# Four graph-attention layers on one core: an opening with gated loads, two reordered rounds, a smaller first piece in layer 3, and POOL converting one adjacency tile

## The reference

```python
x = _layernorm(x + _L0_gnn_ref(x, adj, W, a))          # 4 heads of 64, leaky slope 0.01, then elu
x = _layernorm(x + _L1_gnn_ref(x, adj, W, a1, a2))     # 4 heads of 64, leaky slope 0.2
x = _layernorm(x + _L2_gnn_ref(x, adj, W, ...))        # 1 head of 256, beside three dense branches and a gate
x = _layernorm(x + _L3_gnn_ref(x, adj, 4096, W, b, a)) # weights that depend on the source node alone
```

## Time and profile before

| what | value |
|---|---|
| median of 3 runs | 3027.12 us (3026.69 to 3028.43) |
| profiled execution, time | 3027.04 us |
| profiled execution, span | 3025.2 us |
| granted TensorE clock, mean | 0.992 |
| busy: PE, DVE, ACT, POOL | 2947.3, 2138.8, 1921.5, 1173.2 us |

### The profile page before, as it was taken

The page is one execution under the profiler, slowest core; times in us unless marked ns, Lnnn a source line. Parts: engine busy times, 40 slices in busy tenths (PEclk is TensorE's granted clock), DMA queues, the critical chain, the costliest instruction groups (busy, mean ns, idle before and its releaser), DMA issues.

```text
span 3025.2 us, 65221 instructions
## 1 busy us (share of the span) xinstructions
PE 2947.3 (97%) x24628; PEld 2580.8 (85%) x24628; DVE 2138.8 (71%) x3855; ACT 1921.5 (64%) x3414; POOL 1173.2 (39%) x1559
## 2 busy tenths in 40 slices
PE   7899999999989999999999999999999999989999
PEld 6899999999989999999998877888788878755555
DVE  5998888888988888888886556665666666562245
ACT  4777899999988999999995544454455444430000
POOL 0661385642226656564222023233333333444222
PEclk9999999999999999999999999999999999999999
DMA  8667100000100000000010000000000000000001
GB/s 289 203 206 246 60 15 11 14 11 15 61 12 15 11 11 14 11 14 11 15 34 12 4 1 4 4 1 4 1 4 4 1 1 1 2 1 1 0 14 42
DMA packets 41912, 104.55 MB, mean 35 GB/s; under 512 B 9856, under 2 KB 23424, under 8 KB 33536
## 3 DMA queue, kind: packets, MB, share of 16 engines
q1 hardware_dynamic: 39616, 101.61, 10.3%
q10 hardware_dynamic: 2112, 0.52, 0.1%
HBM read 97.73 MB, written 4.39 MB: 34 GB/s over the span
## 4 chain that ended last, share of the span: by engine, by line
PE 88%; DVE 5%; DMA 3%; ACT 2%; issue 2%; POOL 1%; SPq 0%; DVEq 0%; POOLq 0%; ACTq 0%
PE bank L1373 21%; PE bank L1370 21%; PE bank L1428 15%; PE bank L1466 13%; PE bank L1376 11%; DMA arena<-in_adj_dram 3%; PE bank L1301 2%; PE bank L1455 2%; PE bank L1442 1%; DVE rings L1797 1%; DVE arena L1717 1%; ACT above L967 1%; PE bank L1313 1%; PE bank L1351 1%; DVE rings L1792 1%
## 5 line engine op out<-in xcount | busy, mean ns | idle before, releaser
L1370 PE MATMUL bank<-values,rings 128*128 128x195 bf16 x8192 | 1413.3, 246 | 35.9 <-DVE rings L1800 24.0
L1373 PE MATMUL bank<-values,rings 128*128 128x195 bf16 x8192 | 1413.4, 249 | 0.0
L967 ACT ACTIVATE above<-srow,kpass 128x512 fp8e4<-128x512 f32 x2032 | 1280.1, 709 | 121.3 <-DVE rings L1800 114.6
L1370 PEld LDWEIGHTS bank<-values,rings 128*128 128x128 fp8e4 x8192 | 806.1, 98 | 45.1 <-issue 43.1
L1373 PEld LDWEIGHTS bank<-values,rings 128*128 128x128 fp8e4 x8192 | 788.7, 96 | 0.4
L1797 DVE TENSOR_TENSOR rings<-rings,above 128x512 uint32<-128x512 uint32 x512 | 399.6, 781 | 184.6 <-PE bank L1373 160.9
L1055 ACT ACTIVATE values<-srow,cmul 128x512 f32<-128x512 f32 x256 | 205.8, 814 | 411.2 <-PE bank L1466 410.3
L1800 DVE TENSOR_TENSOR rings<-rings 128x512 uint32<-128x512 uint32 x512 | 430.6, 841 | 17.3
L1466 PE MATMUL bank<-hv,values 128*128 128x257 f32 x1792 | 420.6, 380 | 0.0
L1466 PEld LDWEIGHTS bank<-hv,values 128*128 128x128 f32 x1792 | 335.0, 190 | 69.9 <-issue 25.2
L1376 PE MATMUL bank<-values,rings 128*128 128x390 bf16 x1920 | 320.4, 329 | 11.5 <-DVE values L1833 11.5
(11 more groups left out here) (223 smaller groups left out, 3482.9 us busy)
## 6 DMA issues: line engine op xcount, KB each, us to landing
arena<-in_adj_dram SPq DMA_DIRECT2D x64, 1024.0 KB, 5.0
srow<-src_dram SPq DMA_DIRECT2D x69, 256.0 KB, 3.1
x<-in_x_dram SPq DMA_DIRECT2D x4, 1024.0 KB, 11.4
out_dram<-x SPq DMA_DIRECT2D x7, 512.0 KB, 2.9
arena<-in_L_gnn_fe_w_dram SPq DMA_DIRECT2D x2, 512.0 KB, 6.9
arena<-in_L_gnn_W_hz_dram SPq DMA_DIRECT2D x1, 1024.0 KB, 7.6
arena<-in_L_gnn_g_w_dram SPq DMA_DIRECT2D x1, 1024.0 KB, 10.9
weights<-in_L_gnn_W_dram SPq DMA_DIRECT2D x3, 256.0 KB, 4.0
```

The lines of the kernel that those rows point to most:

```text
L967: last = act.activation(above[:, k % 2, q, :], srow[:, par, :], ACT.Relu, scale=BIG, bias=kpass[:, p % 2, k * Q + q:k * Q + q + 1], satura ...
L1370: pe.matmul(acc[:, 0:KW], pos[:, k % 2, q, :].bitcast(FP8)[:, rows], v[:, 0:KW], start=start, stop=final, skip_group_check=True)
L1373: last = pe.matmul(acc[:, KW:2 * KW], neg[:, k % 2, q, :].bitcast(FP8)[:, rows], v[:, KW:2 * KW], start=False, stop=final, skip_group_chec ...
```

## The change

1. SP's loads of the second to fourth pieces of `x` wait until layer 0's weights have landed.
2. Tile t is packed behind quad t+2 in place of t+1, and the first row goes to bank 6 in place of bank 7.
3. The semaphore of the conversions becomes two, one for each half.
4. In layer 0's first group POOL converts tile 9 (both halves), between its row factors and its wait for the first values; DVE no longer does.
5. In layer 3 the first chunk of 8 tiles is cut into two pieces of 4, and the order of the pieces' steps between the units changes (`FIRST3`). The edge masks of units 0 and 1 are made in DVE's rounds 12 and 13.
6. In the tail of layer 2, ACT copies h of round 2 before the last gate's linear part, and PE multiplies round 2 before the last gate's transposes; rounds 2 and 3 follow in a new order.

```diff
+BY_POOL_TILE = PACKED_FIRST + PACKS - 1
+def first_pieces(l):
+    return [0] + [Q] * (l == 3) + list(range(CHUNK, T + 1, CHUNK))
...
-        s_adjbf = sem("adj_is_bf16")
+        s_adjbf = [sem("adj_is_bf16_0"), sem("adj_is_bf16_1")]
...
                     if t > 0:
-                        sp.wait_ge(s_adjbf, t * 2 + (half - 1))
+                        sp.wait_ge(s_adjbf[half], t)
...
             for i in range(X_PIECES):
+                if i == 1:
+                    sp.wait_ge(s_w, loaded_weights[0])
...
-                j = slice(u * CHUNK, (u + 1) * CHUNK)
+                j = slice(*first_pieces(l)[u:u + 2])
+                at = Q if l == 3 and u == 1 else 0
+                vtmp = vtmp[:, :, at:at + j.stop - j.start]
...
+            def convert(t, half):
+
+                pool.wait_ge(s_adj[half], (t + 1) * 16)
+                pool.wait_ge(s_packmm, t * 2 + half - 3 + CREDIT)
+                pool.tensor_scalar(adj_bf[:, t % 2, half, :], adj_in[:, half, :], 0, None, ALU.is_gt)\
+                    .then_inc(s_adjbf[half], 1)
...
                 if l < 2:
                     row_factors(l)
-                pool.wait_ge(s_vfirst, first_values_before(l) + 2 * FIRST_CHUNKS)
+                if l == 0:
+                    for half in range(2):
+                        convert(BY_POOL_TILE, half)
+                pool.wait_ge(s_vfirst, first_values_before(l) + 2 * len(first_pieces(l)) - 2)
...
                 tanh3(1)
                 gate_tanh(EG - 2)
+                copy_h(2)
                 g_linear(EG - 1)
-                for r in (2, 3):
-                    copy_h(r)
-                    tanh3(r)
-                    copy_xT(r + 2)
+                tanh3(2)
+                copy_xT(4)
+                copy_h(3)
+                tanh3(3)
+                copy_xT(5)
...
-                    if first and k % 2 == 0:
-                        pe.wait_ge(s_vfirst, first_values_before(l) + k + 2)
+                    if first and k * Q in first_pieces(l):
+                        pe.wait_ge(s_vfirst, first_values_before(l) + 2 * first_pieces(l).index(k * Q) + 2)
...
                 g2_product(EG - 2)
+                product3(2)
                 g_across(EG - 1)
-                for r in (2, 3):
-                    product3(r)
-                    across3(r + 2)
+                across3(4)
+                product3(3)
+                across3(5)
...
-                        if l == 0 and 1 <= q <= PACKED_WOVEN:
+                        if l == 0 and 2 <= q <= PACKED_WOVEN + 1:
                             if q == ROW_AT + 1:
                                 pe.wait_ge(s_srow[0], 16)
-                            pack(q - 1)
+                            pack(q - 2)
...
-            FIRST3 = {0: ((first_rests, 0),),
-                      1: ((first_lasts, 0), (first_products, 1), (first_rests, 1), (first_products, 2), (first_lasts, 1)),
-                      3: ((first_rests, 2), (first_products, 3), (first_lasts, 2)),
-                      5: ((first_rests, 3), (first_lasts, 3))}
+            FIRST3 = {0: ((first_rests, 0), (first_lasts, 0), (first_products, 1), (first_rests, 1), (first_products, 2),
+                          (first_lasts, 1)),
+                      1: ((first_rests, 2), (first_products, 3), (first_lasts, 2)),
+                      3: ((first_rests, 3), (first_products, 4), (first_lasts, 3)),
+                      5: ((first_rests, 4), (first_lasts, 4))}
+            def edge_ahead3(k):
+
+                shift = 6 - k
+                dve.wait_ge(s_unit, TURN[3] * H * UNITS + k - 1 + CREDIT)
+                dve.tensor_scalar(edge[:, k], packed[:, :, 0:WORDS], shift, ONE, ALU.logical_shift_left,
+                                  ALU.bitwise_and).then_inc(s_sides, 1)
...
-                        dve.wait_ge(s_unit, unit - 1 + CREDIT)
-                        dve.tensor_scalar(edge[:, r], words, shift[0], ONE, shift[1], ALU.bitwise_and)\
-                            .then_inc(s_sides, 1)
+                        if not first or k >= UNITS_AHEAD:
+                            dve.wait_ge(s_unit, unit - 1 + CREDIT)
+                            dve.tensor_scalar(edge[:, r], words, shift[0], ONE, shift[1], ALU.bitwise_and)\
+                                .then_inc(s_sides, 1)
...
-                        if k < 2 * len(packs_of(g)):
+                        if k < 2 * len(packs_of(g)) and packs_of(g)[k // 2] != BY_POOL_TILE:
                             convert(packs_of(g)[k // 2], k % 2)
...
                     if r == 9:
                         x_norm(EG - 1)
+                    if r in (12, 13):
+                        edge_ahead3(r - 12)
```

More of the change, by code:

```diff
@@ L392, in gnn_kernel @@
             "gate_in", "gate", "parts", "fused", "var", "rstd", "normed", "x"))
+        loaded_weights = [16 * 4, 16 * 13, 16 * 16, 16 * 18]
         block = ctx.enter_context(nc.Block())
@@ L529, in _ @@
             sp.wait_ge(s_out, 16 * (QUADS - 1 + QT))
-        loaded_weights = [16 * 4, 16 * 13, 16 * 16, 16 * 18]
         FOLDS = {1: 2, 2: 9}
@@ L910, in copy_row @@
                 act.wait_ge(s_rowps, l + 1)
-                act.activation(srow[:, 0, :], bank[7][:, :], ACT.Copy).then_inc(s_srow[0], 16)
+                act.activation(srow[:, 0, :], bank[6][:, :], ACT.Copy).then_inc(s_srow[0], 16)
             def above_ahead(l, n):
@@ L1035, in first_casts3 @@
             def first_casts3():
-                for u in range(BITS // 2):
+                for u in range(len(first_pieces(3)) - 1):
                     for i in range(2):
@@ L1307, in pack_half @@
             def pack_half(t, half, b):
-                pe.wait_ge(s_adjbf, t * 2 + half + 1)
+                pe.wait_ge(s_adjbf[half], t + 1)
                 for k in range(half * (BITS // 2), (half + 1) * (BITS // 2)):
@@ L1327, in first_row @@
                 if l == 0:
-                    pe.wait_ge(s_packed, ROW_AT - 1 + CREDIT)
+                    pe.wait_ge(s_packed, ROW_AT - 2 + CREDIT)
                 for it in range(GT):
-                    last = pe.transpose(bank[7][:, it * P:(it + 1) * P],
+                    last = pe.transpose(bank[6][:, it * P:(it + 1) * P],
                                         scores[:, 0, it:it + 1].to_broadcast([P, P]), ident[:, :])
@@ L1717, in convert @@
                 dve.tensor_scalar(adj_bf[:, t % 2, half, :], adj_in[:, half, :], 0, None, ALU.is_gt)\
-                    .then_inc(s_adjbf, 1)
+                    .then_inc(s_adjbf[half], 1)
             def store_packed(t, b):
@@ L1811, in first_products @@
             def first_products(l, u):
-                if l == 3 and u > 0:
+                if l == 3 and u > 1:
                     dve.wait_ge(s_vrest, first_values_before(l) + 2 * u)
@@ L1817, in first_products @@
                     dve.tensor_copy(big[:, :, D:C], factor)
-                    dve.tensor_tensor(big[:, :, 0:D], columns, factor.to_broadcast([P, CHUNK, D]), ALU.mult)\
+                    dve.tensor_tensor(big[:, :, 0:D], columns, factor.to_broadcast([P, columns.shape[1], D]), ALU.mult)\
                         .then_inc(s_vbig, 1)
             def first_rests(l, u):
-                if l == 3 and u > 0:
+                if l == 3 and u > 1:
                     dve.wait_ge(s_vfirst, first_values_before(l) + 2 * u)
```

## The result

The changed kernel takes 3039.0 us (median of 7 runs, 3037.0 to 3039.5); the kernel before, beside it on the same chip, took 3027.6. The ratio is 1.0037 (95% interval 1.0027 to 1.0046): slower by about 11.4 us. I had forecast 3030.5, with a range that ended at 3037.5. The profiled execution took 3038.73, with a span of 3036.7 against 3025.2.

A forecast was written before the change was run, and what follows sets the result against it. The prediction took PE to bound most of the kernel (88% of the chain) and the adjacency stream to bound the opening. Its sum was 3027.04 + 2.0 + 3.3 - 0.7 - 1.1 = 3030.5 us, range 3025.5 to 3037.5.

The forecast's parts named there:

- I take d = 1.7: Layer 0's first group: one POOL conversion of a half tile takes d = 1.7 us, not 5.1.
- The term of 3.3: Layer 0's first group: POOL's two conversions hold DVE, costing +3.3 us, bounds 0 and 9.9.
- The row that decided: Layer 0: beside POOL's supposed one-constant instruction at 78.27, DVE lost only 0.08 us, taken to favour d = 1.7.
- the rule that the two holds together cost 2d - 0.23: Layer 0's first group: POOL's first conversion costs DVE d - 0.23, the second d; 3.3 us in sum.
- POOL is slow and holds DVE: Rival, layer 0's first group: d = 5.1, the group costs 9.9 us, total 3037.1; chance 0.23.
- The opening: +2.0 forecast: Opening: the empty queue makes the adjacency stream start and end 2.0 us later; bounds 1.0 and 3.0.
- The loop of landing and conversion: Opening: each half tile costs a 4.9 us landing and a 1.2 us conversion, whatever PE does.
- dense work that is done sooner buys nothing: Opening: it ends when the adjacency stream ends, so the fold 4.7 us sooner is worth nothing.
- Packing one quad later: 0: Opening: packing tile t behind quad t+2 costs 0, covered by the adjacency stream.
- The saved conversions, 0: Layer 0's first group: DVE loses two conversions of 1.22 us, worth 0 because DVE has slack behind ACT's cast.
- The tail, -0.7: Tail of layer 2: the new order removes ACT's idle before its tanh, -0.7 us; bounds -1.3 and 0.
- Layer 3, -1.1: Layer 3's first group: -1.86 from the smaller piece, +0.5 masks, 0.25 stall; sum -1.1 us, bounds -1.5 and -0.3.

The follow-up runs named there:

- the run in which DVE converts: Changed kernel, but DVE converts both halves of tile 9 as before: 3028.9 us against 3027.0 for the kernel before.
- the seven with this opening: Seven profiled executions with x's wait and later packs, loads by halves; PE's first unit at 75.81 to 77.99 us, 2.8 to 4.9 later than before.
- the quarters: Adjacency loaded and converted by quarters: with only the tail and layer 3 edits 3027.0 us; on changed kernel with DVE converting tile 9, 3029.1; before 3027.0.
- the pieces: Changed kernel with each of POOL's two conversions cut into four of 512 elements: 3029.5 us against 3027.7 for the kernel before.
- no gate: Changed kernel, but x's second to fourth pieces no longer wait for layer 0's weights: 3035.7 us against 3027.0 for the kernel before.
- gate alone: Kernel before, plus only the wait of x's second to fourth pieces for layer 0's weights: 3029.8 us against 3027.0.
- one half: Changed kernel with only tile 9's second half on POOL, the first on DVE: 3033.5 us against 3027.7 for the kernel before.
- the second one of the changed kernel: Profiled execution from measuring the unaltered changed kernel again: median 3037.9 us, five runs 3034.7 to 3041.9, against 3026.5 for the kernel before.
- the packs put back: Changed kernel, but packs behind quad t+1 and first row in bank 7 as before: 3034.0 us against 3027.0 for the kernel before.

## Why the prediction was wrong, step by step

**"I take d = 1.7" is the step that failed.** The place stood: POOL's first conversion got in around the gap of 0.23 us, and its two halves held two-operand instructions of DVE. I took d from the flat slope of a 512-element row of f32 arithmetic because DVE had lost only 0.08 us beside POOL's at 78.27. The row of the same kind (5.1) was the nearer: 5.7. The term of 3.3 (its sum is 3.2) measured 7.4 at tile 10, 6.5 by layer 1 (7.6 against the run in which DVE converts).

The row that decided was misread. POOL's instruction at 78.27 has two constants (`-1.0, 0.0, ALU.mult, ALU.min`), not one, and so has the 512-element row. Its own 1.00 us for 128 elements (0.66 in layer 1) already spoke against the flat slope, which gives 0.34 there. The rows with one constant stand just before it in the same group, at 128 elements 1.40 and 1.10 us (0.90 and 0.54 in layer 1):

```profile
75.03 1.40 POOL L687 TENSOR_SCALAR zrow<-zrow 128x128 f32<-128x128 f32 x1
...
77.19 1.10 POOL L691 TENSOR_SCALAR cmul<-zrow 128x128 f32<-128x128 f32 x1
```

And what DVE loses does not measure how long POOL works: a two-operand instruction came free 3.6 us into POOL's 5.7. So the rule that the two holds together cost 2d - 0.23 failed as well: with d = 5.7 it gives 11.2 for the group.

The rival "POOL is slow and holds DVE" with 3037.1 was the case that came; the rule of the Trainium skill beside it, that the hold is the instruction's, however long, spoke for it, and I gave it 0.23. What no term had foreseen is that POOL's whole work does not set the price but what each single instruction holds: in pieces the same work costs nothing that the medians show, and some 2 us in the trace.

**The opening: +2.0 forecast, +4.2 here.** Fold (9.0 forecast, 8.52), empty queue and first conversion (+2.0, +2.1) were right. "The stream starts 2.0 us later and ends 2.0 us later" was not: two loads in flight fell into long landings, another 2.1 us in this execution; the seven with this opening spread over 2.2. The loop of landing and conversion that I called the bound isn't one, as the quarters show; "dense work that is done sooner buys nothing" held in every run. "Packing one quad later: 0" holds only with the gate.

**The saved conversions, 0:** right (3.05 us of wait; by the medians the pieces and DVE's own conversions end level). **The tail, -0.7:** measured -0.5; the bias sum at 2636.13 took 1.81 us and ate some. **Layer 3, -1.1:** measured -1.0, made of -1.8 up to PE's start (2.84 us against 2.8 forecast), the 0.2 us of issue before it, and 0.6 of stall given back (0.25 forecast).

**The clock had no term.** At layer 2's start PE does the same work after the same waits in both kernels, but takes longer. After:

```profile
1650.57 5.40 PE L1451 MATMUL bank<-arena,powers 128*128 128x257 f32 x12 [0.75 <-ACT powers L1171]
```

and before:

```profile
1639.27 3.72 PE L1428 MATMUL bank<-arena,powers 128*128 128x257 f32 x12 [0.75 <-ACT powers L1150]
```

After, the granted clock was at the lower level (1.2 GHz) from 1650.7 for 3.4 us, which cost 1.7; at layer 1's start the low stretch was 10.2 us in place of 6.8, which cost 0.6 by layer 2's start. PE's idle ahead of it is the same in both (0.55, 0.46 and 0.75 us). The low stretch at layer 2's start is there in four profiled executions (changed, no gate, gate alone, one half), the same four in which that at layer 1's start is 10.2 us; in the other ten, the second one of the changed kernel among them, it is missing, and the one at layer 1's start is 6.8. What decides it stays open; so does whether the packs put back are truly 4 to 5 us better than the changed kernel. With d = 5.7 by the prediction's rule (11.2) the sum would have been 3038.4, near the result, but by errors that cancel: the group cost less than that and the opening more.

## What to carry to other kernels

Before work is moved to POOL, its duration is taken from a row of the same operation and the same kinds of data, since size and slope of another operation say little; and the question is not how busy POOL is but how long one of its instructions is, and what DVE does at that moment. If the work must go there, cut it: here eight instructions of 1.6 us cost some 2 us in the trace, and nothing that the medians show, where two of 5.7 cost 7.6. A gate that lets a small transfer pass ahead of a big one costs an empty queue, here 2.1 us, on a stream whose engines are busy nearly all the time, whatever it gives the engine behind it.

## What the runs showed of the hardware

- POOL, 2048 elements of int32 to bf16: copy 2.05 us, comparison with one constant 5.5 to 5.9, with a second constant 7.3; 512 elements with one constant 1.5 to 1.8.
- A one-operand DVE instruction is held by POOL as well (conversion 1.22 to 6.40, mask 0.42 to 7.30), until some 0.15 us before POOL's own end when its duration alone is taken off. A two-operand one came free sooner: beside the comparison it could have started 3.6 us into POOL's 5.7 (92.69 + 3.84 - 0.69 - 92.21), with two constants 4.5 into 7.3, beside the copy 1.9 into 2.05, and three more passed while POOL was still at work. The Trainium skill's "SBUF — State Buffer", section "Who interferes with whom", agrees on the first: a tensor_scalar or copy of DVE in a two-port mode blocks for the whole instruction. It says that two SBUF inputs clash with POOL's reads; that POOL's reads end ahead of its writes would fit the second, but no run here shows which of the two it was doing.
